# First expert layer: the last two blocks of the always-on expert computed as three fp32r products, with the second block's first products moved ahead

## The reference, cut to what matters

```
logits = xf @ Wg
top_vals, top_idx = jax.lax.top_k(logits, TOP_K)
top_w = jax.nn.softmax(top_vals, axis=-1)
...
h = jax.nn.relu(jnp.einsum('td,edf->tef', xf, W1) + b1)
sparse = jnp.einsum('te,tef,efd->td', combine, h, W2)
sparse = sparse + combine @ b2
shared = jax.nn.relu(xf @ Ws1 + bs1) @ Ws2 + bs2
out = sparse + shared
```

## Time and profile before

| what | value |
|---|---|
| median of three runs | 1574.87 us (1573.02 to 1576.65) |
| profiled execution | 1576.46 us, span 1574.4 us |
| TensorE busy in the span | 1388.0 us (88%) |
| DVE, ACT, POOL busy | 676.0, 661.1, 504.9 us |
| end of the ring, last block of the phase, start of the next phase | 597.6, 664.7, 668.1 us |

### The profile page before, as it was taken

The page is one execution under the profiler, slowest core; times in us unless marked ns, Lnnn a source line. Parts: engine busy times, 40 slices in busy tenths (PEclk is TensorE's granted clock), DMA queues, the critical chain, the costliest instruction groups (busy, mean ns, idle before and its releaser), DMA issues. The chain is left out here.

```text
span 1574.4 us, 29080 instructions
## 1 busy us (share of the span) xinstructions
PE 1388.0 (88%) x9586; PEld 1119.9 (71%) x9587; DVE 676.0 (43%) x2234; ACT 661.1 (42%) x1482; POOL 504.9 (32%) x563
## 2 busy tenths in 40 slices
PE   4999988999999999799997899957588898867698
PEld 3666765699999996567775799954365676645587
DVE  4666724300000005367752500035853563538485
ACT  3355543144444442246663244433344444326452
POOL 4356541022222221033321022215327744123430
PEclk9799998999999999979998999987889999989799
DMA  8500006455656554000003655630036875010000
GB/s 284 163 2 1 2 1 197 139 184 197 205 192 212 191 180 124 0 14 15 15 15 95 217 181 191 207 108 1 1 143 212 278 229 173 16 53 1 1 27 27
DMA packets 114271, 176.90 MB, mean 112 GB/s; under 512 B 20571, under 2 KB 90861, under 8 KB 113529
## 3 DMA queue, kind: packets, MB, share of 16 engines
q1 hardware_dynamic: 103999, 147.40, 29.3%
q0 software_dynamic: 10176, 28.24, 5.1%
HBM read 136.21 MB, written 39.35 MB: 112 GB/s over the span
## 5 line engine op out<-in xcount | busy, mean ns | idle before, releaser
L1442 ACT ACTIVATE kT<-ps,b_sb 128x128 f32<-128x128 f32 x312 | 114.8, 368 | 155.6 <-PE ps L1557 134.7
L718 ACT ACTIVATE wbuf<-ps 128x512 f32<-128x512 f32 (+1 forms) x256 | 123.6, 542 | 84.8 <-PE ps L963 84.3
L1557 PEld LDWEIGHTS ps<-qT,wbuf 128*128 128x128 f32 x1248 | 145.4, 192 | 3.9 <-issue 1.9
L1557 PE MATMUL ps<-qT,wbuf 128*128 128x128 f32 x1248 | 145.7, 275 | 1.7 <-issue 1.7
L1567 PE MATMUL ps<-L0f_second,kT 128*128 x624 | 141.1, 379 | 0.0
L277 POOL TENSOR_TENSOR sm<-sm,mhalf 128x4 f32<-128x4 f32 (+1 forms) x40 | 41.9, 1048 | 276.1 <-DVE sm L272 276.1
L1567 PEld LDWEIGHTS ps<-L0f_second,kT 128*128 128x128 f32 x624 | 115.5, 190 | 14.1
L963 PE MATMUL ps<-nmT_r,sel_r 32*128 32x256 f32 (+1 forms) x512 | 110.0, 426 | 0.0
L765 DVE CUSTOM_DVE_ANT_0 ps<-ps,ts 128x128 f32<-128x128 f32 (+1 forms) x256 | 83.1, 390 | 44.8 <-PE ps L939 44.8
L768 DVE TENSOR_REDUCE nmax<-ps 128x2 f32<-128x512 f32 x128 | 80.4, 683 | 31.9 <-PE ps L939 31.7
L1968 ACT ACTIVATE kT<-ps,b_sb 128x128 f32<-128x128 f32 x152 | 55.6, 368 | 72.8 <-PE ps L2055 62.8
(11 more groups left out here) (455 smaller groups left out, 3138.4 us busy)
## 6 DMA issues: line engine op xcount, KB each, us to landing
wbuf<-in_L_w SPq DMA_DIRECT2D x66, 1024.0 KB, 5.1
tree_rows<-rt SPq DMA_DIRECT2D x3, 3151.0 KB, 23.0
prob<-tree_rows SPq DMA_DIRECT2D x69, 137.0 KB
tree_outputs<-probT SPq DMA_DIRECT2D x69, 128.0 KB
L0f_second<-in_L_w SPq DMA_DIRECT2D x8, 1024.0 KB, 11.4
ts<-in_L_b SPq DMA_DIRECT2D x58, 128.0 KB, 2.9
wbuf<-in_L_rec SPq DMA_DIRECT2D x3, 2048.0 KB, 9.0
expert_rows<-vbuf SPq DMA_DIRECT2D x2, 2048.0 KB, 10.0
```

The costliest lines, as they stand in the source:

```text
L718: act.activation(PT[:, k, :, q0:], ps[:, a_bank("ST", b, k), :].rearrange("p (h s) -> p h s", h=2)[:, :, q0:], ACT.Exp, scale=scale).then_ ...
L1442: act.activation(hs[:, f, :], hidden(f), func, bias=b1_sb[:, v, f:f + 1]).then_inc(h_in, 1)
L1557: ins = pe.matmul(hidden(f), first[v][:, kk, f * P:(f + 1) * P], xgT[:, kk, :], start=(kk == 0), stop=(kk == KD - 1))
```

## The change

Blocks 2 and 3 of the shared expert are computed from split operands. A float32 value is rounded to fp32r (the high part); the rest is subtracted exactly (the low part). Three fp32r products, high by high, low by high and high by low, take the place of one float32 product. The routed results are fetched into another buffer, since the old one now holds the high weights.

* In the ring, ACT rounds the shared weights in four pieces after steps 2 to 5, DVE subtracts the four low pieces, ACT rounds the first block's inputs after step 6 and POOL subtracts their low part after step 10.
* In each block ACT takes a hidden tile out (`raw`) and copies it rounded (`hh`); POOL subtracts (`hl`, line 1418 of the changed file). `low_rows` and `low_hidden` are POOL's new instructions.
* The second block's first products stand ahead of token block 1's turning and of the fold; its second products stand behind them.

The diff, cut to its core:

```
-            gat = [prob[:, :, :, :, :].rearrange("p a b c s -> p (a b c) s"), probT[:, :, :, :].rearrange("p a b s -> p (a b) s")]
+            gat = [wbuf[:, 1, v * 2048:(v + 1) * 2048].rearrange("p (t d) -> p t d", d=D) for v in range(2)]
...
+                        if isinstance(s, int) and 2 <= s < 6:
+                            q = chunk(s - 2)
+                            dve.wait_ge(w_hi, s - 1)
+                            dve.tensor_tensor(wbuf_r[0][:, q], wbuf[:, 0, q], hi_room[:, q], ALU.subtract).then_inc(w_lo, 1)
...
+                    def low_rows(i):
+                        pool.wait_ge(x_hi, i + 1)
+                        pool.tensor_tensor(xl[i], xnT[:, :, block_of(i)], xh[i], ALU.subtract).then_inc(x_lo, 1)
+
+                    def low_hidden(i, fs):
+                        for f in fs:
+                            pool.wait_ge(hid_hi, i * NF + f + 1)
+                            pool.tensor_tensor(hl[:, f, :], raw[:, f % 4, :], hh[:, f, :], ALU.subtract).then_inc(hid_lo, 1)
...
+                        if s == 10:
+                            low_rows(0)
                     if shared:
+                        low_hidden(0, range(NF))
                         for i in range(3):
...
-                    for blk in range(NB):
-                        nrm.power(pool, blk, 0)
+                    nrm.power(pool, 0, 0)
+                    low_rows(1)
+                    low_hidden(1, range(3))
+                    nrm.power(pool, 1, 0)
+                    low_hidden(1, range(3, NF))
+                    nrm.power(pool, 2, 0)
+                    nrm.power(pool, 3, 0)
...
+                        if isinstance(s, int) and 2 <= s < 6:
+                            q = chunk(s - 2)
+                            act.wait_ge(s_full, 2 * lead)
+                            act.activation(hi_room[:, q], wbuf[:, 0, q], ACT.Identity).then_inc(w_hi, 1)
+                        if isinstance(s, int) and s == 6:
+                            act.activation(xh[0], xnT[:, :, block_of(0)], ACT.Identity).then_inc(x_hi, 1)
+
+                    def split_block(i):
+                        for f in range(NF):
+                            act.wait_ge(h_full, (lead + steps + i) * NF + (f + 1))
+                            wait(act, hid_lo, i * NF + f - 3)
+                            act.activation(raw[:, f % 4, :], ps[:, f % 4, :], func, bias=col("L0_bs1", f)).then_inc(h_in, 1)
+                            act.wait_ge(h_in, (lead + steps + i) * NF + (f + 1))
+                            act.activation(hh[:, f, :], raw[:, f % 4, :], ACT.Identity).then_inc(hid_hi, 1)
+                        if i == 0:
+                            act.activation(xh[1], xnT[:, :, block_of(1)], ACT.Identity).then_inc(x_hi, 1)
...
+                    def split_hidden(i):
+                        u = lead + steps + i
+                        pe.wait_ge(x_lo, i + 1)
+                        pe.wait_ge(w_lo, 4)
+                        for f in range(NF):
+                            if f >= 4:
+                                pe.wait_ge(h_in, u * NF + (f - 3))
+                            for k in range(KD):
+                                for j, (w, x) in enumerate(((hi1, xh[i]), (hi1, xl[i]), (lo1, xh[i]))):
...
+                    def split_second(i):
+                        for tp in range(2):
+                            pe.wait_ge(s_in, (lead + i) * 2)
+                            for t in range(2):
+                                for f in range(NF):
+                                    if tp == 0 and t == 0:
+                                        pe.wait_ge(hid_lo, i * NF + (f + 1))
+                                    for j, (h, w) in enumerate(((hh, hi2), (hh, lo2), (hl, hi2))):
...
-                    for blk in range(NB):
-                        if shared and blk % 2 == 0:
-                            shared_block(lead + blk // 2, lead + steps + blk // 2, hT)
-                        if shared and blk == 2:
-                            fold()
-                        norm_T(blk)
+                    if shared:
+                        split_hidden(0)
+                        split_second(0)
+                        norm_T(0)
+                        split_hidden(1)
+                        norm_T(1)
+                        fold()
+                        split_second(1)
+                        norm_T(2)
+                        norm_T(3)
```

More of the change, by code:

```diff
@@ L1090, in phase_experts, with chunk, block_of @@
             b2_sb = ts
+            w_hi, w_lo, x_hi, x_lo = (psem(n + x) for x in ("w_hi", "w_lo", "x_hi", "x_lo"))
+            hid_hi, hid_lo = psem(n + "hid_hi"), psem(n + "hid_lo")
+            hi_room = nc.alloc_sbuf_tensor_at(f"{n}high", [P, 4096], F32R, offset=places["prob"])[:, :]
+            (hi1, lo1) = (x[:, 0:2048].rearrange("p (k f) -> p k f", k=KD) for x in (hi_room, wbuf_r[0]))
+            (hi2, lo2) = (x[:, 2048:4096].rearrange("p (f d) -> p f d", f=NF) for x in (hi_room, wbuf_r[0]))
+            hh, hl = (x.rearrange("p (f t) -> p f t", f=NF) for x in (wbuf_r[2], hbuf_r))
+            raw = attw[:, 0].rearrange("p w k n -> p (w k n)").rearrange("p (i t) -> p i t", i=4)
+            xh = [x.rearrange("p (k t) -> p k t", k=KD) for x in (rounded("rowsF", 4 * D, 1024), rounded("qT", 0, 1024))]
+            xl = [x.rearrange("p (k t) -> p k t", k=KD) for x in (rounded("stage", 0, 1024), rounded("kT", 0, 1024))]
+            def chunk(j):
+                return slice(j * 1024, (j + 1) * 1024)
+            def block_of(i):
+                return slice((lead + i) * BLK, (lead + i + 1) * BLK)
             def hidden(f):
@@ L1515, in shared_block @@
                                                     w2[0][:, f, :], start=(f == 0), stop=(f == NF - 1))
+                            ins.then_inc(s_full, 1)
+                    def split_hidden(i):
[7 more added lines that the diff above has]
+                                for j, (w, x) in enumerate(((hi1, xh[i]), (hi1, xl[i]), (lo1, xh[i]))):
+                                    ins = pe.matmul(ps[:, f % 4, :], w[:, k, f * P:(f + 1) * P], x[:, k, :],
+                                                    start=(k == 0 and j == 0), stop=(k == KD - 1 and j == 2))
+                            ins.then_inc(h_full, 1)
+                    def split_second(i):
[6 more added lines that the diff above has]
+                                    for j, (h, w) in enumerate(((hh, hi2), (hh, lo2), (hl, hi2))):
+                                        ins = pe.matmul(ps[:, 4 + tp, t * D:(t + 1) * D], h[:, f, (2 * tp + t) * P:(2 * tp + t + 1) * P],
+                                                        w[:, f, :], start=(f == 0 and j == 0), stop=(f == NF - 1 and j == 2))
                             ins.then_inc(s_full, 1)
```

14 lines of the change are left out of this document (7 added, 7 removed).

## The result

| | before | changed kernel |
|---|---|---|
| median, first comparison | 1576.76 us (6 runs) | 1589.16 us (6 runs), ratio 1.007, 95% interval 1.0052 to 1.0089 |
| median, repeated later | 1577.48 us (24 runs) | 1587.33 us (6 runs), ratio 1.0058, 1.0043 to 1.0073 |
| profiled execution, span | 1576.46, 1574.4 us | 1589.81, 1587.7 us |

The change makes the kernel 0.6 to 0.7% slower, 9 to 11 us by the ratios; 5.1 us were forecast. The direction was right, the size was not, and the measured time lies outside the range.

A forecast was written before the change was run, and what follows sets the result against it. The end of the second block's second product was taken to bound the phase: 10.4 us saved on TensorE, 15.5 spent ahead, 5.1 later, so 1574.87 + 5.1 = 1580.0 us. Forecast's own range 1578 to 1582.6; wider range 1573.5 to 1582.6.

The forecast's parts named there:

- The exclusion: POOL subtractions and DVE instructions with both inputs in SBUF alternate; a pair takes 1.46 us, DVE losing about 1.05.
- step 2: Combine 0 on DVE meets POOL's subtractions, starting at 605.98 and ending at 614.0 us instead of 609.4.
- step 5: Combine 1 and norms 1: `power` 1 queues on POOL behind low tiles 0 to 2 and ends at 630.7 us.
- step 7: TensorE: turning 1 waits for line 286 until 636.3, the fold ends about 641.9, then 4.8 us wait for `s_in`.
- step 9: Second block's second product ends at 660.3 us (before 655.2), from 646.7 + 11.5 + 2.1; the phase ends 5.1 us later.
- B: Rival, milder stall: line 286 free or the clock kept, 1575.5 to 1578 us; 22%.
- C: Rival: DVE and POOL do not exclude each other here; 1573.9 us with half clock, 1571.0 with clock kept; 18%.
- E: Rival: weight loads hold three products to before's 14 us, about 1583, 3%. As a point: second block's second product ends.
- D: Rival: POOL worse than priced, for instance both delayed by full instructions, or ACT held by `hid_lo`; 1583 to 1587 us, 7%.
- the last step: The phase's 5.1 us carried to the whole kernel: 1581.6 against the profiled execution, 1580.0 against the median 1574.87.
- step 8: TensorE has little work from 633.2 to 646.7 us; 4.4 us at half clock lose 2.1; dense work restores the clock.

The follow-up runs named there:

- f4_fill: Changed kernel with POOL's 16 subtractions of the hidden low parts replaced by fills with zero; 1578.85 us, ratio 1.0004 to the kernel before.
- g1_before_194: Kernel before with 194 idle instructions on TensorE behind the second expert ring; 1581.68 us, ratio 1.0016.
- g2_after_62: Changed kernel with 62 idle instructions on TensorE behind the second expert ring; 1585.11 us, ratio 1.0039 to the kernel before.
- f2_after_pad: Changed kernel with 126 idle instructions on TensorE behind the second expert ring; 1583.11 us, ratio 1.0035 to the kernel before.
- e1_late: Kernel before with twelve extra unread statistics instructions on DVE ahead of the phase's last norm, a 4.5 us delay; 1584.02 us, ratio 1.0029.
- g3_all_62: Changed kernel: first block's shared results read before combine 2, `power` 1 before low tiles, turning 1 and fold last, 62 idle instructions; 1577.08 us, ratio 0.9987.
- g4_old_order: Changed kernel with before's order on TensorE and ACT, `power` 1 ahead of the second block's low tiles, 62 idle instructions; 1578.68 us, ratio 1.0007.
- e3_power: Changed kernel with `power` 1 ahead of all low tiles of the second block; 1587.80 us, ratio 1.0043 to the kernel before.
- h2_all_warm: g3_all_62 with 14 unread matmuls in TensorE's wait ahead of the second block's second product, idle instructions cut to 34; 1576.22 us, ratio 0.9985.

## Why the prediction was right and wrong

**Right, by its own steps.** The exclusion (step 2: 8.0 us forecast for combine 0, 7.9 measured; f4_fill takes it away and gets 3.4). Line 286 alternates too: 3.47 and 5.21 us instead of 1.38. `power` 1 stands behind tiles (step 5; 628.9 to 629.9, forecast to end at 630.7). The wait for `s_in` is 4.80 us (step 7: 4.8); both its ends came 1.1 us earlier than forecast, so that the tenth agrees is luck. The half clock there costs 2.6 us: the second product took from 645.62 to 659.7, 14.1 us instead of the 11.5 of step 9 (forecast 2.1 more). From the ring's start the next phase began 4.9 us late, 5.1 were forecast. Rivals B, C and E of the prediction fell: no milder stall, no freedom from exclusion, three products at their price (11.0 us for the 16 threes of the first block's first product, forecast 10.9). D had a time above the forecast, but its mechanism, POOL worse than priced, didn't occur: five contended tiles took 6.42 us, 1.28 each, where 1.46 were priced.

**Wrong: the last step.** "Against the profiled execution (1576.46) that makes 1581.6" carried a loss at one phase unchanged to the end, and so put everything behind the phase at nothing, without a reason. Three things stood in its way.

1. The code behind. The 194 instructions that the change adds to TensorE moved a 16 KB transfer of code onto the last store of the tree ring, at 1328.5 us. It costs about 3 us; that the place of the code does it is shown in both directions by g1_before_194, g2_after_62 and f2_after_pad. No term of the sum and no rival had it.
2. The clock behind the phase. The fall to 0.50 was costed where it was seen, up to E. By then the clock was back (1.00 from 655.0 to 659.7); it fell again between the last turnings, as before, and then stayed down longer. Before, it was back at 0.99 some 3.9 us into the next phase, and step 8 read this as what dense work does. In the changed kernel the same work had 0.50 for 13.2 us and 0.66 for the next 19, and 1.6 us were lost up to the second ring. What decides it isn't settled. e1_late, a mere delay, had 0.50 and 0.67 and lost 1.4 us. f4_fill, locally earlier than before, had 0.50 and 0.66 and lost as much as the changed kernel. g3_all_62, 3.2 us shorter locally, had 0.63 and 0.71 and lost 1.6, and f2_after_pad, the same program as the changed kernel up to there, had 0.63 and 0.70 and lost 0.2. And as e1_late lost 4.6 us in all, this is the least certain of the three.
3. The base. 1574.87 us was the median of three runs; over the comparisons since, the kernel before had medians of 1576.8 to 1579.2 us. Two of the 9.2 us between 1580.0 and 1589.16 are this.

4.9 + 1.6 + 3 make 9.5 us, beside the 9 to 11 measured by the ratios (12.4 by the medians of the first comparison, 9.9 by those of the second). What remains, up to 1.5 us by the ratios and up to 3 by those medians, isn't assigned. The first term is shown by the traces and the edits; the second is one row of single profiles, the third an estimate. The range was too narrow for the same reason: its upper bound held only local terms.

**What the order is worth.** The prediction blamed the subtractions for `s_in`, rightly, and took the moved order as given. g4_old_order shows that three products in the old order lose 0.8 us locally and tie in time, so of the 4.9 us about 4 come from moving the second block's first products ahead; the place of `power` 1 makes no difference that shows in the new order (e3_power, 359.0 against 358.6). The order isn't bad for TensorE; it puts eight low tiles onto L286 and combine 2. The best version, g3_all_62 (or h2_all_warm), keeps the three products, is 3.2 us shorter locally, and measures 0.13% (0.15%) faster than before, with intervals that end at 1.0.

## What to carry to other kernels

Where two engines exclude each other, moving TensorE's work earlier moves the other engines' work too, so ask which instructions will then run beside each other; a gap on TensorE can be what keeps them apart, and filling it made this kernel 0.3% slower. A change that adds instructions shifts where code blocks are fetched in all that follows: before a few microseconds far away are explained by the change, add idle instructions to the engine until the added ones make a multiple of 256 (194 and 62 here), and look again. And a local loss isn't carried to the end as it is: give the range a term for the clock of the next phase and for the code behind.

## What was not expected of the hardware

* One 16 KB packet of code on one DMA engine made a store of 128 KB land 1.7 us later (1.9 to 3.6 us from its issue) where a load of a megabyte was issued 0.4 us behind it. Whether the load is needed for this was not tested.
* A normalising instruction with one tensor operand takes 3.46 us for four beside a single 2.4 us POOL subtraction, and 1.38 alone; beside POOL fills DVE's `combine` loses nothing, while the normalising instruction lost 0.47 us beside one.
* 18 matmuls that TensorE was given to hold the clock took 7.23 us at a mean clock of 0.56 instead of 4.1, so they ran 3.2 us beyond the wait that they filled.
